# Workspace FFN, the last stage of a decoder: output-bias additions at the step's beginning, TensorE's filling products spread over other places, LayerNorm moments taken one step ahead, and attention scores in the order of A's chunks

## What is computed

```python
z = layernorm(x)                        # input of the layer; result is x + out
ws = workspace                          # 16 slots x 512
for _ in range(2):                      # two blocks
    logits = rms(z, norm_pre) @ compete_w.T + compete_b
    vals, idx = top_k(logits.T, 4)      # per slot, 4 of 128 tokens
    written = softmax(vals) @ (z @ write_w.T + write_b)[idx]
    ws = rms(ws + written, norm_post)
    k, v = ws @ wk.T + bk, ws @ wv.T + bv
    att = softmax((z @ wq.T + bq) @ k.T / 8)      # 8 heads, 16 slots
    z = rms(z + (att @ v) @ out_w.T + out_b, norm_post)
```

## Time and profile before

| | before |
|---|---|
| median of 3 runs | 4096.97 us (4094.72 to 4097.59) |
| the profiled execution | 4095.58 us, of which span 4093.8 us |
| the last layer's first matmul | 3054.8 us from the span's start |
| TensorE busy in the span | 3644.9 us (89%) |
| VectorE, ScalarE, POOL busy | 2875.2 (70%), 2573.2 (63%), 1785.7 us (44%) |
| mean granted TensorE clock | 0.965 of full speed |

### The profile page before, as it was taken

How to read it: one execution, slowest core, us unless ns; L and a number is a source line. 1 busy time by engine, 2 the same in 40 slices (tenths; PEclk the granted TensorE clock), 3 DMA queues, 4 the chain that set the end, 5 groups by cost and what they waited for, 6 DMA issues and landing times. The chain is left out here.

```text
span 4093.8 us, 86187 instructions
## 1 busy us (share of the span) xinstructions
PE 3644.9 (89%) x24323; PEld 1810.7 (44%) x24323; DVE 2875.2 (70%) x4470; ACT 2573.2 (63%) x6419; POOL 1785.7 (44%) x2216
## 2 busy tenths in 40 slices
PE   5999999999999994899999799999958878888886
PEld 1222222222222221778778444444436555465563
DVE  5888888888888883677777577777744454444545
ACT  2777777777777774677777577777734434344352
POOL 6444444444444430666665122222222543545535
PEclk9999999999999997899999999999979999999998
DMA  7777777777777762333332233333340120211102
GB/s 115 121 125 120 124 122 123 124 120 125 122 120 125 121 94 85 101 113 112 114 114 87 78 94 94 93 95 95 94 141 1 47 78 2 88 38 62 63 1 78
DMA packets 342548, 385.78 MB, mean 94 GB/s; under 512 B 58432, under 2 KB 223040, under 8 KB 342336
## 3 DMA queue, kind: packets, MB, share of 16 engines
q1 hardware_dynamic: 315712, 348.69, 39.4%
q10 hardware_dynamic: 26624, 34.63, 3.3%
HBM read 196.52 MB, written 84.93 MB: 69 GB/s over the span
## 5 line engine op out<-in xcount | busy, mean ns | idle before, releaser
L302 DVE TENSOR_REDUCE a_neg_max<-a_max_ps 128x2 f32<-128x1024 f32 x1024 | 1201.0, 1219 | 194.6 <-PE a_max_ps L354 169.8
L380 ACT ACTIVATE a_P<-a_ring_ps 128x512 f32<-128x512 f32 x2048 | 1084.6, 604 | 382.0 <-PE a_ring_ps L336 378.2
L354 PE MATMUL a_max_ps<-a_K,a_Q 96*128 96x512 bf16 x2048 | 621.1, 385 | 44.0 <-DMA a_K<-a_k_split 39.8
L336 PE MATMUL a_ring_ps<-a_Q,a_K 98*128 98x512 bf16 x2048 | 617.5, 382 | 5.7 <-DMA a_Q<-a_max_rows 3.5
L365 PE MATMUL a_pv_ps<-a_P,a_V 128*32 128x512 f32 x4096 | 544.9, 604 | 1.8 <-ACT a_out_sb L385 1.8
L336 PEld LDWEIGHTS a_ring_ps<-a_Q,a_K 98*128 98x128 bf16 x2048 | 158.9, 96 | 659.5 <-ACT a_P L380 585.5
L1163 ACT ACTIVATE c_P<-c_s_ps,c_bias 128x128 f32<-128x128 f32 x1024 | 361.5, 367 | 138.9 <-DVE c_bias L1035 130.2
L1092 PE MATMUL c_s_ps<-c_KD,c_qT 128*128 128x512 f32 x512 | 276.7, 622 | 33.5 <-ACT c_qT L1154 28.3
L1834 ACT ACTIVATE d_junk<-d_y 128x512 bf16<-128x512 f32 x128 | 80.6, 630 | 341.7 <-DVE d_y L1524 341.7
L256 POOL TENSOR_SCALAR a_var_eps<-a_mean_var 128x1 f32<-128x1 f32 x64 | 12.2, 190 | 648.1 <-DVE a_mean_var L318 647.9
L1031 DVE TENSOR_REDUCE c_neg_max<-c_s_ps 128x4 f32<-128x512 f32 x256 | 175.4, 685 | 163.7 <-PE c_s_ps L1093 163.7
(11 more groups left out here) (240 smaller groups left out, 7187.5 us busy)
## 6 DMA issues: line engine op xcount, KB each, us to landing
a_Q<-a_q_split SPq DMA_DIRECT2D x384, 128.0 KB
a_K<-a_k_split SPq DMA_DIRECT2D x384, 128.0 KB
heads_out<-a_out_sb ACTq DMA_DIRECT2D x128, 256.0 KB, 2.3
a_x_in<-in_x_dram SPq DMA_DIRECT2D x64, 256.0 KB, 3.6
a_c_in<-in_ctx_dram SPq DMA_DIRECT2D x64, 256.0 KB
a_cT_in<-in_ctxT_dram SPq DMA_DIRECT2D x64, 256.0 KB
b_x_in<-in_x_dram SPq DMA_DIRECT2D x64, 256.0 KB, 2.7
b_o_in<-heads_out SPq DMA_DIRECT2D x64, 256.0 KB
```

The source lines that it names most:

```text
L302: dve.tensor_reduce(neg_max[:, p, 2 * u:2 * u + 2], max_ps[u % 2][:, :, :], AX.X, ALU.max, negate=True).then_inc(max_taken, 1)
L336: pe.matmul(ring(s, use_of(k))[:, :], K[i][:, h, n:n + 128], Q[i][:, h, :], start=True, stop=True).then_inc(scores_filled, 1)
L354: last = pe.matmul(max_ps[u % 2][:, j, :], Q[i][0:KROW, h, m:m + 128], K[i][0:KROW, h, :], start=True, stop=True)
L380: act.activation(P[p][k // NT][:, k % NT, :], ring(s, use_of(k))[:, :], ACT.Exp, scale=SCALE).then_inc(exp_done, 1)
```

## The change

Four things move in `workspace_ffn`. No arithmetic is added or taken away.

1. **POOL**: when f is a second block (kinds 2 and 3, eight of sixteen steps that finish a unit), the first six `add_bias` of u stand behind the rms of f and ahead of the two attention normalisations; the last two stand behind them.
2. **TensorE and ScalarE**: `value_out(3)`, `mix(2)` go ahead of the transposition of the top-k weights, `mix(6)` ahead of the workspace transposes, `mix(7)` ahead of the key product; ScalarE copies values(3), values(4) before squares(1), and values(5) and values(7) move in the same way. On VectorE `final(6)` and `residual(7)` go ahead of the addition of the key bias (kd), and `final(7)` ahead of that of the value bias (vd).
3. **VectorE**: the moments of a first block are taken at the end of the step before; four of its batches are normalised before `softmax(0)`, four between the softmax halves.
4. **Scores** run chunk by chunk over four batches, and wait for three chunks of A (six copies), then for the fourth. Chunks 0 and 2 use the SC banks, 1 and 3 the F banks, where it was the other way round.

```diff
-                if u.exists():
+                early = NB - 2 if f.exists() and f.second() else 0
+                if u.exists():
+                    for b in range(early):
+                        add_bias(u, b)
                     for half in range(2):
...
-                    add_bias(u, 0)
-                    add_bias(u, 1)
+                    add_bias(u, early)
+                    add_bias(u, early + 1)
                 for b in range(NB):
-                    if u.exists() and b >= 2:
+                    if u.exists() and early + 2 <= b:
                         add_bias(u, b)
...
+                def normalise(batches):
+
+                    dve.wait_ge(rstd_done, f.eight() + 1)
+                    for b in batches:
...
                 if first:
-
-                    e = f.eight()
-                    dve.wait_ge(x_loaded[f.pair()], f.turn() * 128 + 128)
...
+                    normalise(range(0, NB // 2))
                 if u.exists():
                     softmax(0)
                 if first:
...
+                    normalise(range(NB // 2, NB))
                 if u.exists():
                     softmax(1)
...
                 if u.exists():
                     final(5)
                     residual(6)
+                    final(6)
+                    residual(7)
                 if f.exists():
                     n = f.n()
                     dve.wait_ge(kv_filled, n * 2 + 1)
...
-                if u.exists():
-                    final(7)
+                if after.exists() and not after.second():
+                    moments_of(after)
...
-                        pe.wait_ge(a_done, n * 2 * CK + 2 * CK)
-                        for b in range(half * 4, half * 4 + 4):
-                            for c in range(CK):
+                        for c in range(CK):
+                            pe.wait_ge(a_done, n * 2 * CK + (8 if c == 3 else 6))
+                            for b in range(half * 4, half * 4 + 4):
...
-                        pair = SC if c % 2 else [bank(pe, f, U_A + c + h) for h in range(2)]
-                        if c == 3:
-                            pe.wait_ge(a_done, n * 2 * CK + 4)
+                        pair = [bank(pe, f, U_A + c - 1 + h) for h in range(2)] if c % 2 else SC
+                        if c == 2:
+                            pe.wait_ge(a_done, n * 2 * CK + 2)
```

More of the change, by code:

```diff
@@ L1353, in _, with step @@
                 sp.sem_inc(out_stored[i], 16)
-            def step(f, u):
+            def step(f, u, after):
                 if u.exists() and u.second():
@@ L1489, in _, with moments_of, step @@
             LINKS = 6
-            def step(f, u):
+            def moments_of(f):
+                e = f.eight()
+                dve.wait_ge(x_loaded[f.pair()], f.turn() * 128 + 128)
+                at_least(dve, z_done, e * NB)
+                at_least(dve, x_ms_done, f.n())
+                for b in range(NB):
+                    dve.bn_stats(stats[:, b, :], X[f.pair()][:, b, :]).then_inc(stats_done, 1)
+                for b in range(NB):
+                    held.wait_ge(stats_done, e * NB + (b + 1))
+                    dve.bn_aggr(moments[:, b, :], stats[:, b, :]).then_inc(moments_done, 1)
+            moments_of(Unit(0, 0, 0))
+            def step(f, u, after):
                 def link(k, ins):
@@ L1554, in step @@
                 if first:
-                    dve.wait_ge(rstd_done, e + 1)
-                    for b in range(NB):
-                        dve.tensor_scalar(X[f.pair()][:, b, :], X[f.pair()][:, b, :], moments[:, b, 0:1], rstd[:, b:b + 1],
-                                          ALU.subtract, ALU.mult).then_inc(z_done, 1)
+                    normalise(range(NB // 2, NB))
                 if u.exists():
@@ L1642, in step @@
                 if u.exists():
-                    final(6)
-                    residual(7)
+                    final(7)
                 if f.exists():
@@ L1740, in step @@
                     mix(1)
+                    value_out(3)
+                    mix(2)
                 if f.exists():
@@ L1745, in step @@
                 if u.exists():
-                    value_out(3)
-                    mix(2)
+                    value_out(4)
                 if f.exists():
@@ L1756, in step @@
                 if u.exists():
-                    value_out(4)
                     mix(3)
@@ L1780, in step @@
                     value_out(7)
+                    mix(6)
                 if f.exists():
@@ L1787, in step @@
                 if u.exists():
-                    mix(6)
+                    mix(7)
                 if f.exists():
@@ L1901, in step @@
                     values(6)
+                    values(7)
                     squares(5)
-                    values(7)
                 if f.exists():
```

30 lines of the change are left out of this document (12 added, 18 removed).

## The result

| | before | after |
|---|---|---|
| median of 5 runs | 4096.97 us (4094.72 to 4100.78) | 4119.15 us (4114.91 to 4120.80) |
| ratio to before, 95% interval | | 1.0051 [1.0036, 1.0066] |
| span of the profiled execution | 4093.8 us | 4113.1 us |
| the last layer's first matmul | 3054.8 us | 3057.4 us |
| TensorE busy | 3644.9 us | 3635.6 us |

The changed kernel is slower by 0.51%: 22 us against the 4114.0 - 4097.0 = 17 us that were forecast. The whole interval lies above the 0.2% that stands for no change. The layer's first matmul is 2.6 us later, and no edit lies ahead of it.

A forecast was written before the change was run, and what follows sets the result against it. TensorE must be kept fed, with ten us a step of waits. Terms 30 + 11.4 - 20.8 - 12.6 - 10 + 17.7 + 2.1 = +17.8 us on 4095.58 give 4113.4, stated as 4114, range 4082 to 4137.

The forecast's parts named there:

- attention weights late, and the clock: Kinds 2 and 3: six early bias additions make attention weights late, +30 us; lower TensorE clock behind, +11.4 us.
- L: The time in a step at which TensorE transposes the logits (L1729), directly behind the transposes of the attention weights.
- POOL gives back in kind 3, with scores: Steps 3, 7, 11: bias additions gone from between POOL's batches give back 6.3 us each, 7.2 with scores' 0.9.
- the same in step 15: Step 15, written out: POOL gives back only 1.9 us, as VectorE's chain stays slow beside POOL's addition.
- moments and split: Kinds 0 and 1: split normalisation and later load of X delay attention weights 3.2 or 2.7 us a step, +17.7.
- vd +2.1: Kind 0: the value bias addition behind final(7) frees its bank late, costing 0.7 us in three steps, +2.1.
- The scores by chunks: Start of scores: TensorE's wait of 1.19 us falls to about 0.3, 0.9 us in 14 steps, -12.6.
- The products: Kinds 1 and 2: wait for top-k weights moves to gT; mix(6) and clock leave 1.25 us a step, -10.
- A: Rival, faster: residual(3) comes earlier, TensorE keeps a pair of 2.1 us in 16 steps, -33.6, so 4080; chance 0.10.
- B: Rival, no change: clock stays up, attention weights less late; 4103 us (0.20) or 4073 us (0.05); chance 0.25.
- D: Rival: chunk order gives nothing, 4127 us; or low clock in kinds 0 and 1, 4123 us; chance 0.10 together.
- C: Rival, slower: POOL additions and VectorE softmax subtractions block each other, +11.2 us in eight steps, 4125 us; chance 0.15.

The follow-up runs named there:

- e4: The kernel before with the six early bias additions alone, placed as in the change: 4113.43 us, ratio 1.0039 to the kernel before.
- e6: The kernel before with moved products, values, finals, residuals and moments alone, one normalisation: 4083.13 us, ratio 0.9964 to the kernel before.
- e1: The changed kernel without its early bias additions, the three other parts kept: 4087.69 us, ratio 0.9976 to the kernel before.
- e5: The kernel before with scores by chunks and the swapped banks alone: 4086.29 us, ratio 0.9965 to the kernel before.
- e9: The changed kernel with four output buffers in place of two, one scratch tile fewer on ScalarE: 4114.84 us, ratio 1.0041 to the kernel before.
- e2: The changed kernel with all eight normalisations behind softmax(0) again: 4106.24 us, ratio 1.0027 to the kernel before.
- e3: The changed kernel with the six early additions ahead of POOL's wait for the squares of X: 4059.91 us, ratio 0.9913 to the kernel before.

## Why the prediction was right

The forecast was 4114, slower, and the median is 4119.15, in the range. The profiled execution took 4114.91, against a sum of 4113.4. Term by term, from the table:

| term | predicted | measured |
|---|---|---|
| attention weights late, and the clock (ahead of L, kinds 2, 3) | +41.4 | +44.2 |
| POOL gives back in kind 3, with scores (steps 3, 7, 11) | -21.6 | -15.3 |
| the same in step 15 | -2.8 | -3.9 |
| moments and split (ahead of L, kinds 0, 1) | +17.7 | +16.5 |
| behind L, kind 0 (scores -2.7, vd +2.1) | -0.6 | -1.6 |
| behind L, the other eight (scores, products) | -15.4 | -20.2 |

(The scores' 0.9 are dealt out by steps; one of the 14 lies ahead of this stretch, so the column adds up to 18.7 and not 17.8.)

**Late attention weights: right in all, wrong in its parts.** Outside the branch L slips by 6.6 us a step against 4.5 + 1.9 = 6.4. But the addition row starts 9.8 us behind the score start and not 8.2: POOL's rms of X comes 1.0 later in the step, and there is a gap of 0.7 that I had left out. The 1.0 is a price of the chunk order that the prediction didn't have: in step 7 the rms stands 6.50 us behind the score start before, and in e4 and e6, which keep the old order, and 7.48 in e1 and e5, which have the new one. The reason is argued only: the scores start sooner, and ScalarE's squares, which stand behind its copies of A, do not. So the lateness is 6.2 us, and of the clock only 0.4 falls ahead of L. The rest of the lower level's price is behind L: 1.94 - 1.06 = 0.9 for the first value_out product. In steps 6 and 10, behind the branch, it is 4.5 and 3.4 against 1.5: the slack behind the branch is there (2.1 and 3.2 less than 6.6), but the 1.7 of POOL's later start come on top. In 14 and 15 it is 5.0.

**What POOL gives back: the mis-sized term.** The prediction said "Together -20.8". e1 against the change says 12.2 in kind 3 and 1.1 in step 15, 13.3 in all. With the bias additions out of the way, VectorE's finals wait for the store of their buffer, 2.5, 0.9 and 2.0 us in step 7. Most of that wait would have passed anyway: y_r is out at 3516.10 + 0.55 = 3516.65, and the final starts at 3517.21, 0.56 later. But by then POOL's addition is running, and the final takes 0.87 us more than 0.75. Together that is 1.4 us, and these y_r follow each other by 3.6 and 5.0 us in turn, not by 3.6 each. I had read the batch interval of kind 2 (3.57) into kind 3 without asking who frees the buffer that a final writes. e9 takes the stores away and gets 4.1 of the missing 6 in kind 3. The 3.57 is the figure that was mis-sized.

**The scores by chunks**: predicted 12.6, measured alone 12.8. That the two agree so well is luck: the term was a shorter wait in 14 steps, and e5 shows 16.6 gained behind L, 11.2 lost again ahead of it in kinds 0 and 1, and a median some 7 us lower than these places explain.

**The products: right mechanism, too small a size.** w_top and ws fell as said, and a wait for gT came, but it is 28.5 us in ten, up to 4.3, where I had said 1 to 2 each. Against that, ws fell in all kinds and not in kind 3 alone. Alone, with the moments, the part gives 16 us and not 8 (10, less the 2.1 for vd). The nine steps that are neither of kind 3 nor 0 give 9.9 of it behind L; the rest is what kinds 0 and 1 gain ahead of L beyond what kd and vd cost.

**The moments and the split: right.** Of 17.7, 13.2 were for the split (e2: 10.9 in the steps, 12.9 in the medians) and 4.5 for the later load (129.4 - 123.8 = 5.6). What the prediction didn't have is that this load couples all terms: e5 gains 16.6 behind L and loses 11.2 in kinds 0 and 1. The parts alone, with the split from e2, come to -12.8 - 15.9 + 15.0 + 12.9 = -0.8, and the change to +20.9 (0.51% of 4098). In the change's own table the terms do add up, to +19.4, in the places where the prediction has them.

Two errors cancelled: the additions cost 10.9 more than the 20.6 that I had for them (31.5), and the rest gave 10.8 where I had 2.8. That late attention weights make the kernel slower is the mechanism as predicted, and e1, e3 and e4 show it; that the sum came within 5 us of the median is in part luck.

**The rivals.** A needed gT waits under 1 us, and they are 2.9 on average. B needed the clock to stay up: it was 0.50. D needed the chunk order to give nothing: e5. Its second half, a low clock in kinds 0 and 1, is there, but was there before: 32 transposes of X take 3.53 + 2.02 = 5.55 us behind the wait of 5.42, and took 5.68 in step 8 of the kernel before.

C did not come where it was priced, for a reason that the timeline shows: the softmax subtraction, the only operation of VectorE there with two inputs in SBUF, ends at 3489.15 in step 7, and the first addition starts at 3489.39. All 18 subtractions of the stretch take 0.69 us but for one of 0.82. Where the two do meet the price is there, and it is part of what kind 3 did not give back. The final at 3517.21 starts 0.19 us behind POOL's addition of the input and takes 1.62 in place of 0.75: it ends 0.55 behind that addition's end (3518.28). The Trainium skill ("SBUF — State Buffer", section "Who interferes with whom") has the two engines lock each other out for a whole instruction when VectorE reads two inputs in SBUF and GpSimd reads SBUF too; the trace agrees at 3517.21 to 0.2 us: a final held until the addition's end would end at 3519.03, and this one ends at 3518.83.

## What to carry to other kernels

An instruction that is moved ahead to fill an idle engine must stand ahead of the wait it is to fill. Ahead or behind was 59 us here, with the same six additions, and the trace of before shows both places: 11.75 us idle in front of the rms, and 3.69 behind it. When a wait is taken away, ask who frees the buffers and loads the data that the faster chain will use. The early load alone was worth 26 us here; four output buffers in place of two gave 4, which is not clear of noise. Parts that share one such slack don't add up, so price each with the others in place.

## What was not expected of the hardware

The lower clock level doesn't cost these groups twofold. Eight value_out products took 1.94 us at 0.50 and 1.06 at 1.00, four transposes 1.11 and 0.66, two 0.63 and 0.38: factors of 1.83, 1.68 and 1.66. Behind the wait of 5.75 us in step 7 the level lasted some 5 us, and what ran in it lost 0.45 + 0.45 + 0.25 + 0.88 us, and 0.18 in the mix behind it (1.30 for 1.12), together 2.2 us of work, of which only 0.4 shows ahead of L.

A wait need not be as long as that. In step 1 of the kernel before, eight value_out products behind an idle time of 2.02 us and one transpose took 1.94 us too, at a granted clock of 0.50 from 3122 to 3124.
